# Attention of a gated cross-attention block in half-precision pairs, exponentials head by head in 5 of 8 tiles, and one reordering in the gate phase

## The chip, the cores and the metric

The kernel runs on one core of one Trainium2 chip. The time is the device time of that core in microseconds (us). TensorE does matmuls and transposes, VectorE and ScalarE read what it leaves in PSUM, GpSimd works from SBUF alone, and SyncE issues the DMAs. In the rows they are PE (its weight loads PEld), DVE, ACT, POOL and SP.

## What is computed

The reference, cut to what matters. B = 4 batches of S = 1024 tokens, hidden size 512, 16 heads of 64; the context has 64 rows, so a token scores 16 x 64 = 1024 context entries.

```
def attention(query, key, value, w_q, w_k, w_v, w_o):
    q, k, v = (split_heads(t @ w) for t, w in ((query, w_q), (key, w_k), (value, w_v)))
    scores = jnp.einsum('bhqd,bhkd->bhqk', q, k) * HEAD_DIM ** (-0.5)
    scores = scores + (1.0 - mask)[None, None, :, :] * -10000.0      # causal
    weights = jax.nn.softmax(scores, axis=-1)
    return merge_heads(jnp.einsum('bhqk,bhkd->bhqd', weights, v)) @ w_o

def ffn(x, w_gate, w_up, w_down):       # x and every intermediate rounded to 16-bit steps
    up, gate = act_qdq(x @ lpbq_dequant(w_up).T), act_qdq(x @ lpbq_dequant(w_gate).T)
    o = act_qdq(act_qdq(gate * fixed_qdq_u16(sigmoid(gate))) * up)
    return o @ lpbq_dequant(w_down).T   # lpbq_dequant: 4-bit steps, blocks of 32

x = x + tanh(g_xattn) * attention(layernorm(x), ctx, ctx, w_q, w_k, w_v, w_o)
x = x + tanh(g_ffn) * ffn(layernorm(x), w_gate, w_up, w_down)
```

## The kernel before

There are four phases one behind the other, with a barrier or a grid-wide maximum between them: front (attention), gate, up, down. Each product is made of three matmuls in which both factors are split in a high and a low part (high x high, high x low, low x high). In the front the parts are fp32r, in the other phases fp16.

**Front.** The 4096 tokens are 32 tiles of 128 (index j, eight to a batch). Key weights times query weights are folded into A (512 x 1024), value weights times output weights into V, once for a batch; `Ah`, `Al`, `Vh`, `Vl` are their parts. All engines walk the same list of steps k (`schedule`), three of them software-pipelined over the tiles:

- PE in step k: eight transposes of the probabilities of tile k-2 into `pT` (L987), the 24 matmuls of the scores of tile k (L956), four transposes of the normalised input of tile k+1 (L974), and the 24 matmuls of the output of tile k-2 (L925). In steps 8 and 9 of a batch the A and V of the next batch are made between these (L891, L905).
- ACT in step k: `pTh` of tile k-2 (L631), the normalisation of tile k+2 (L616), one exponential over 128x1024 of tile k-1 (L655), `xh` of tile k+1 (L662), and the second normalisation of tile k-3.
- DVE in step k, inside a run of batches: statistics of tile k+2 (L750), `pTl` of tile k-2 (L798), largest score of each head of tile k-1 (L740), scores minus largest (L744), residual and its statistics for tile k-3 (L761, L767), sums of the exponentials (L775) and their reciprocals (L778), `xl` of tile k+1 (L859), largest of tile k-3 (L782). In the last batch the residual and its statistics come ahead of the largest score.
- POOL in step k: inverse deviations (L584 to L589), then probabilities of tile k-1 (L601).

Besides, four of the weight tiles of the gate matrix are dequantised in each of the first three batches (jobs q = 0 to 3). `job_scale` (DVE, L282 to L274) runs in steps 3 to 6, behind `xl`; `job_integer` (DVE, L324) and `job_turn` (PE, L333) in steps 4 to 7, `job_turn` behind `xl` of tile k+1; `job_hi` (ACT) and `job_lo` (DVE) in steps 5 to 8. PE may overwrite the scores in `pS` of tile k-2 when DVE has subtracted (`sub_done`). DVE, ACT and PE take their instructions strictly in this written order.

**Gate.** Four groups of 1024 tokens, each with two halves t of 12 products `it` of 12 matmuls (L1278). ACT empties each product (L1171), DVE takes its minimum and maximum (L1202, L1203). The weight tiles of the other matrices are dequantised meanwhile, one for each four products: at `it == 9` DVE runs `job_scales` for three coming tiles (L296 to L274), which is followed by `job_integer` of the tile in hand (L324); PE turns that tile behind product 11 (L333), which waits for it. `job_scales` runs in seven of the eight halves.

**Up and down** are not touched.

Of the kernel before, what the change touches and what calls it, by code (L numbers as in the profile page):

```python
# [26 lines left out]
P = 128  # L27
# [39 lines left out]
def flamingo_block(nc, x, ctx, g_xattn, g_ffn, w_q, w_k, w_v, w_o, w_gate, w_up, w_down, out):  # L67
# [22 lines left out]
    with ExitStack() as top:  # L90
# [49 lines left out]
        with ExitStack() as ff:  # L140
# [12 lines left out]
            with ExitStack() as early:  # L153
                Ah = sb(early, "Ah", [P, KT, INNER], F32R)
                Al = sb(early, "Al", [P, KT, INNER], F32R)

# [31 lines left out]

ROUNDS = 4


# [188 lines left out]
def front_phase(mk, xf, cf, weights, shared, g_xattn, g_ffn, w_src, w_dst, load_gate, unit, xr, xr_in, front_out, pS, pG, x1_d, xn_d, ident, mask, half,  # L380
# [13 lines left out]
    with ExitStack() as ph:  # L394
        xin = [sb(ph, f"xin{n}", [P, H], F32) for n in range(BQ)]
        xn = [sb(ph, f"xn{n}", [P, H], F32) for n in range(2)]
        xh = [sb(ph, f"xh{n}", [P, H], F32R) for n in range(2)]
        xl = [sb(ph, f"xl{n}", [P, H], F32R) for n in range(2)]
        pr = [sb(ph, f"pr{n}", [P, INNER], F32) for n in range(2)]
        pTh = sb(ph, "pTh", [P, INNER], F32R)  # L400
        pTl = sb(ph, "pTl", [P, INNER], F32R)
        x1 = [sb(ph, f"x1{n}", [P, H], F32) for n in range(2)]
# [8 lines left out]
        ssum = sb(ph, "ssum", [P, 2, HEADS], F32)  # L411
        srec = sb(ph, "srec", [P, 2, HEADS], F32)
        pT = pb(ph, "pT", 1024)
        pX = pb(ph, "pX")
# [10 lines left out]
        Vh = sb(ph, "Vh", [P, PAIRS, H], F32R)  # L425
        Vl = sb(ph, "Vl", [P, PAIRS, H], F32R)
        pw = [pS[0][:, 0:512], pS[0][:, 512:1024]]
# [14 lines left out]

        kbd_set, vb_set = sem("kbd_set"), sem("vb_set")
        apart_p, apart_e = sem("apart_p"), sem("apart_e")
        masked, apart, sx_red, sx_spread, sx_scale = (sem(n) for n in ("masked", "apart", "sx_red", "sx_spread", "sx_scale"))
# [164 lines left out]
        def _(act):  # L610
# [7 lines left out]
            def step(b, k, have, jobs):  # L618
# [7 lines left out]
                if have(k - 2):  # L626
                    j = k - 2
                    act.wait_ge(*tile(o_ps, b, j - 1))
                    for h, cs in enumerate(halves):
                        act.wait_ge(*part(pT_ps, b, j, h))  # L630
                        act.activation(pTh[:, cs], pT[:, cs], ACT.Copy).then_inc(pTh_done, 1)  # L631
                if q is not None and which != 0:
                    job_hi(act, J, b, q)

                def chunk_high(n):
                    act.wait_ge(*at(ch_ps, NCH * b, NCH * ahead + 8 * which + n + 1))
                    if which == 0:
                        act.activation(Ah[:, n // 2, halves[n % 2]], bank_of(k, 0, n), ACT.Copy, scale=SCALE).then_inc(ch_hi, 1)
                    else:
                        act.activation(Vh[:, block_of(n), :], bank_of(k, 1, n), ACT.Copy).then_inc(ch_hi, 1)  # L640

# [9 lines left out]
                def exponentials():  # L651
                    if have(k - 1):
                        j = k - 1
                        act.wait_ge(*tile(sub_done, b, j))
                        act.activation(pr[j % 2][:, :], pr[j % 2][:, :], ACT.Exp).then_inc(exp_done, 1)  # L655

                def high():
                    if have(k + 1):
                        j = k + 1
                        act.wait_ge(*tile(xT_ps, b, j))  # L660
                        act.wait_ge(*tile(s_ps, b, j - 2))
                        act.activation(xh[j % 2][:, :], pX[:, :], ACT.Copy).then_inc(xh_done, 1)  # L662

# [46 lines left out]
        def _(dve):  # L710
            def chunk_low(b, k, ahead, which, n):
                dve.wait_ge(*at(ch_hi, NCH * b, NCH * ahead + 8 * which + n + 1))
                bank = bank_of(k, which, n)
                if which == 0:
                    cs = halves[n % 2]
                    dve.scalar_tensor_tensor(out=Al[:, n // 2, cs], in0=bank, scalar=SCALE, in1=Ah[:, n // 2, cs].bitcast(F32),
                                             op0=ALU.mult, op1=ALU.subtract).then_inc(ch_lo, 1)
                else:
                    q = block_of(n)
                    dve.tensor_tensor(Vl[:, q, :], bank, Vh[:, q, :].bitcast(F32), ALU.subtract).then_inc(ch_lo, 1)  # L720

            def scores_down(b, j, between=lambda: None):
# [4 lines left out]
                dve.wait_ge(*tile(s_ps, b, j))  # L727
                dve.wait_ge(*part(pT_ps, b, j - 2, 1))
# [27 lines left out]
            def residual(b, j):  # L756
# [3 lines left out]
                dve.wait_ge(*tile(x2_done, b, j - 2))  # L760
                dve.scalar_tensor_tensor(out=x1[n][:, :], in0=pO[:, :], scalar=TG_X, in1=xin[j % BQ][:, :],  # L761
                                         op0=ALU.mult, op1=ALU.add).then_inc(x1_done, 1)
# [9 lines left out]
            def sums(b, j):  # L772
                n = j % 2
                dve.wait_ge(*tile(exp_done, b, j))
                dve.tensor_reduce(ssum[:, n, :], pr[n][:, :].rearrange("p (h c) -> p h c", c=CK), X, ALU.add).then_inc(sum_done, 1)  # L775
                dve.wait_ge(*tile(sum_done, b, j))
# [3 lines left out]
            def largest(b, j):  # L780
                dve.wait_ge(*tile(x2_done, b, j))
                dve.tensor_reduce(xmx[:, bass.ds(BQ * b + j, 1)], x2[j % 2][:, :], X, ALU.max,  # L782
                                  apply_absolute_value=True).then_inc(x2max_done, 1)

            def step(b, k, have, jobs):
# [7 lines left out]
                def lows():  # L793
                    if have(k - 2):
                        j = k - 2
                        for h, cs in enumerate(halves):
                            dve.wait_ge(*part(pTh_done, b, j, h))
                            dve.tensor_tensor(pTl[:, cs], pT[:, cs], pTh[:, cs].bitcast(F32), ALU.subtract).then_inc(pTl_done, 1)  # L798

# [15 lines left out]

                q = job_at(k, jobs, 2)
                if which == 0:
                    sums_up()
# [36 lines left out]
                if have(k + 1):  # L855
                    j = k + 1
                    dve.wait_ge(*tile(xh_done, b, j))
                    dve.wait_ge(*tile(s_ps, b, j - 2))
                    dve.tensor_tensor(xl[j % 2][:, :], pX[:, :], xh[j % 2][:, :].bitcast(F32), ALU.subtract).then_inc(xl_done, 1)  # L859
                some(8)  # L860
                q = job_at(k, jobs, 0)
                if q is not None:
                    job_scale(dve, J, b, q, unit[:, 3 * q + b:3 * q + b + 1])
                if have(k - 3):
                    largest(b, k - 3)

            for j in range(2):
                statistics(0, j)
            schedule(dve, step, straight=True)

# [10 lines left out]
        @block.tensor  # L881
        def _(pe):
            def keys(b, k, ahead, n):

                pe.wait_ge(*at(ch_lo, NCH * b, NCH * ahead + n - 3))
                if n == 0:
                    pe.wait_ge(kbd_set, 2 * b + 2 * ahead + 2)
                    pe.wait_ge(*tile(sub_done, b, k - 2))
                for q in range(4):
# [20 lines left out]
            def values(b, k, have, turn_x):  # L910
# [7 lines left out]
                for i in range(PAIRS):  # L918
# [18 lines left out]
                    if which == 1 and i % 2 == 1:  # L937
                        if i == 3:

                            pe.wait_ge(*tile(sub_done, b, k - 1))  # L940
                        four_heads(b, k, ahead, i // 2)

            def scores(b, k):
                pe.wait_ge(*tile(xl_done, b, k))
                pe.wait_ge(*tile(sub_done, b, k - 2))
                if k % BQ == 2:

                    pe.wait_ge(*at(ch_lo, NCH * b, NCH * (k // BQ) + NCH))
                for kt in range(KT):
# [4 lines left out]
                    for xs, As in ((xh, Ah), (xh, Al), (xl, Ah)):  # L954
                        for hf in range(2):
# [3 lines left out]
                                           stop=(kt == KT - 1 and xs is xl))  # L959
                mm.then_inc(s_ps, 1)  # L960

            def step(b, k, have, jobs):
# [30 lines left out]
                if k % BQ != 2 and not (which == 0 and have(k - 2)):  # L993
                    turn_x()
                values(b, k, have, turn_x)
                if which == 0:
                    scores(b, k)
# [36 lines left out]
            for r in range(ROUNDS):  # L1034
                project(wv, r, wv_in, [(k_sb, 3 + r)] if r < 2 else [(v_sb, r - 1)], v_ps)
            schedule(pe, step)

# [9 lines left out]
def gate_phase(mk, xn_d, xr, xr_in, front_out, pX, x_d, x_pair, gate_d, wsc, w_src, W, w_in, load_w, row_unit, row_scale, ident, S_X, INV_X, GPOS, GNEG):  # L1047
# [3 lines left out]
    with ExitStack() as ph:  # L1051
# [133 lines left out]
        def _(dve):  # L1185
# [668 lines left out]
```

## Time and profile before

| | us |
|---|---|
| median of 3 runs | 1414.65 |
| lowest, highest | 1409.73, 1418.82 |
| the profiled execution | 1419.34 |
| its span in the profile | 1417.6 |

| engine | busy, us | share of the span |
|---|---|---|
| PE | 1288.8 | 91% |
| PEld | 768.2 | 54% |
| DVE | 1008.7 | 71% |
| ACT | 663.8 | 47% |
| POOL | 243.2 | 17% |

All times of rows are of one profiled execution, counted from the start of its span. A matmul's duration (390 to 417 ns for 512 columns) is longer than the distance to the next one, since matmuls are pipelined; for what one costs, take the distance of starts. An ACTIVATE too starts before the record of the one ahead has ended. "x2" in a row means two instructions merged, with their joint duration.

### The profile page before, as it was taken

To read this page: it belongs to the slowest core of one execution; us is meant where nothing else is said; L and a number is where in the kernel's file an instruction comes from. 1 tells how busy PE (TensorE), PEld (TensorE's weight loads), DVE (VectorE), ACT (ScalarE), POOL (GpSimd) and SP (SyncE) were. 2 spreads that over 40 slices of the span, in tenths; PEclk is the share of its full clock that TensorE was granted. 3 is DMA by queue.
4 is the path that set the end of the run, shared out by engine and by line. 5 is a ranking of instruction groups with operands and counts; after the bars stand their busy time and mean duration, and the time that the engine had idled before them with its cause. 6 is when DMAs were issued, how large, how long until landed. Compare 5 with 4: busy or idle time off the path is not lost. (4 is left out here: it accounts for less than half of the span.)

```text
span 1417.6 us, 19287 instructions
## 1 busy us (share of the span) xinstructions
PE 1288.8 (91%) x6269; PEld 768.2 (54%) x6269; DVE 1008.7 (71%) x1465; ACT 663.8 (47%) x782; POOL 243.2 (17%) x331
## 2 busy tenths in 40 slices
PE   7899999999999989899998999999993039999998
PEld 6688868878878754444444444444441014444443
DVE  0478779878876656666656669997999994545554
ACT  3434344443443223333333268875677984343431
POOL 1124234324313221110011113210110000000000
PEclk9999999999999999999999999999997569999999
DMA  8013212212203355545553489974457863454543
GB/s 326 1 34 94 83 52 75 96 44 83 95 37 105 119 191 181 166 168 192 170 178 119 159 298 351 322 282 146 140 195 299 314 245 126 164 180 155 183 158 116
DMA packets 111244, 228.28 MB, mean 161 GB/s; under 512 B 23121, under 2 KB 35409, under 8 KB 111185
## 3 DMA queue, kind: packets, MB, share of 16 engines
q1 hardware_dynamic: 110896, 227.58, 46.8%
q8 instruction: 26, 0.43, 0.1%
q14 instruction: 34, 0.27, 0.1%
q10 hardware_dynamic: 288, 0.00, 0.0%
HBM read 136.32 MB, written 91.23 MB: 161 GB/s over the span
## 5 line engine op out<-in xcount | busy, mean ns | idle before, releaser
L1278 PE MATMUL gpG<-xph,Wh 128*128 128x512 f16 x384 | 149.3, 389 | 1.1 <-DVE xpl L1189 1.0
L1278 PE MATMUL gpG<-xpl,Wh 128*128 128x512 f16 x384 | 149.2, 388 | 0.0
L1278 PE MATMUL gpG<-xph,Wl 128*128 128x512 f16 x384 | 148.7, 387 | 0.0
L1801 PE MATMUL pD<-Wh,xph 128*128 128x512 f16 x384 | 145.5, 379 | 1.0 <-DVE xpl L1776 1.0
L1278 PE MATMUL pU<-xph,Wh 128*128 128x512 f16 x384 | 145.5, 379 | 0.0
L1278 PE MATMUL pU<-xpl,Wh 128*128 128x512 f16 x384 | 145.5, 379 | 0.0
L1278 PE MATMUL pU<-xph,Wl 128*128 128x512 f16 x384 | 145.5, 379 | 0.0
L1801 PE MATMUL pD<-Wl,xph 128*128 128x512 f16 x384 | 145.5, 379 | 0.0
L1801 PE MATMUL pD<-Wh,xpl 128*128 128x512 f16 x384 | 145.5, 379 | 0.0
L1171 ACT ACTIVATE gst<-gpG,rw 128x512 f32<-128x512 f32 x96 | 66.2, 689 | 161.8 <-PE gpG L1278 161.8
L1202 DVE TENSOR_REDUCE gmx<-gst 128x512 f32 (+1 forms) x96 | 65.6, 684 | 97.9 <-ACT gst L1171 97.7
L925 PE MATMUL pO<-Vh,pTh 128*128 128x512 f32 x256 | 106.7, 417 | 3.5 <-DVE pTl L798 2.3
L925 PE MATMUL pO<-Vh,pTl 128*128 128x512 f32 x256 | 101.3, 396 | 0.0
L925 PE MATMUL pO<-Vl,pTh 128*128 128x512 f32 x256 | 101.1, 395 | 0.0
L956 PE MATMUL pS<-Ah,xh 128*128 128x512 f32 x256 | 81.7, 400 | 1.7 <-DVE Vl L720 1.7
L956 PE MATMUL pS<-Al,xh 128*128 128x512 f32 x256 | 79.4, 391 | 0.0
L956 PE MATMUL pS<-Ah,xl 128*128 128x512 f32 x256 | 79.0, 390 | 0.0
L631 ACT ACTIVATE pTh<-pT 128x512 fp32r<-128x512 f32 x64 | 34.8, 597 | 93.0 <-PE pT L987 93.0
L1419 ACT ACTIVATE gb<-nq,sc 128x1536 f32<-128x1536 int16 x48 | 75.2, 1568 | 4.4 <-POOL nq L1399 4.2
L1292 PE MATMUL pD<-ident 128*128 128x512 f16 x28 | 7.9, 446 | 75.5 <-DVE pmx L1714 75.5
L601 POOL TENSOR_TENSOR pr<-pr,srec 128x1024 f32<-128x1024 f32 x32 | 61.0, 1906 | 72.8 <-DVE srec L778 72.4
L655 ACT ACTIVATE pr<-pr 128x1024 f32<-128x1024 f32 x32 | 33.9, 1060 | 82.9 <-DVE pr L744 62.2
(222 smaller groups left out, 2639.5 us busy)
## 6 DMA issues: line engine op xcount, KB each, us to landing
dub<-up_d SPq DMA_DIRECT2D x42, 768.0 KB, 4.8
gate_d<-gst SPq DMA_DIRECT2D x96, 256.0 KB, 2.0
gb<-gate_d SPq DMA_DIRECT2D x24, 768.0 KB, 6.5
up_d<-ust SPq DMA_DIRECT2D x72, 256.0 KB, 4.2
eu<-up_d SPq DMA_DIRECT2D x22, 768.0 KB, 6.1
xr<-xn_d SPq DMA_DIRECT2D x9, 1024.0 KB, 6.0
xin<-in_x SPq DMA_DIRECT2D x32, 256.0 KB, 2.8
x_d<-x SPq DMA_DIRECT2D x32, 256.0 KB, 2.0
```

The source lines that it names most:

```text
L601: pool.tensor_tensor(p3, p3, srec[:, j % 2, :].unsqueeze(2).to_broadcast([P, HEADS, CK]), ALU.mult).then_inc(prob_done, 1)
L631: act.activation(pTh[:, cs], pT[:, cs], ACT.Copy).then_inc(pTh_done, 1)
L655: act.activation(pr[j % 2][:, :], pr[j % 2][:, :], ACT.Exp).then_inc(exp_done, 1)
L925: mm = pe.matmul(pO[:, :], ps_[:, cs], vs[:, p, :], start=(i == 0 and ps_ is pTh and vs is Vh), stop=(i == PAIRS - 1 and ps_ is pTl))
L956: mm = pe.matmul(pS[k % 2][:, hf * 512:(hf + 1) * 512], xs[k % 2][:, cs], As[:, kt, hf * 512:(hf + 1) * 512], start=(kt == 0 and xs is xh ...
L1171: act.activation(stage[n][:, :], pG[m % 3][:, :], ACT.Copy, scale=row_scale[0][:, it:it + 1]).then_inc(g_sb, 1)
L1202: dve.tensor_reduce(gmx[:, 1, bass.ds(2 * IT * i + m, 1)], stage[m % NS][:, :], X, ALU.min).then_inc(g_neg, 1)
L1278: mm = pe.matmul(ps[:, :], Ws[:, it, kt * P:(kt + 1) * P], xs[:, kt, :], start=(kt == 0 and Ws is Wh and xs is xh), stop=(kt == KT - 1 and ...
L1292: pe.matmul(ps, words[:, 0:P], words.unsqueeze(1).to_broadcast([P, 2, 2 * P]), start=True, stop=True)
L1419: act.activation(gb[k % NG][:, :], nq[:, k % QT, :], ACT.Sigmoid, scale=S_G).then_inc(sig_done, 1)
L1801: mm = pe.matmul(pD[4 * t + q][:, :], os_[n][:, cs], Ws[:, it, :], start=(it == 0 and os_ is oh and Ws is Wh), stop=(it == IT - 1 and os_ ...
```

## The change

1. `Ah`, `Al`, `Vh`, `Vl`, `xh`, `xl`, `pTh`, `pTl` become fp16. So that they fit, each is multiplied by a power of two: x by 2^10, probabilities by 2^14, A and V by 2^15 over a power-of-two unit that bounds their largest possible entry. The scale is undone in the scale of the exponential (`S_UNIT`) and of the residual (`O_SCALE`). The subtractions on DVE become `scalar_tensor_tensor` with the same operands.
2. The units are found at the start: `largest_of` (DVE) over `wq`, `kT`, `wo`, `vT`, `spread_bounds` (PE, two small transposes each), and `fit_in`, `fit_a`, `fit_v`, chains of ten and nine small DVE instructions. The first high part of A and of V waits for them.
3. In tiles 2 to 6 of each batch (steps 3 to 7) DVE no longer subtracts and no longer sums: it takes the negated largest scores, multiplies these 16 columns by `S_UNIT`, and ACT runs 16 exponentials of 128x64 from `pS`, each with a column of bias, a column of scale, and a sum over its head (`accum_out`). PE overwrites `pS` only when these are done.
4. In the gate phase `job_integer` runs at `it == 9` without `job_scales` ahead of it; `job_scales` moves to `it == 10`.

```
+X_TOP, P_TOP, M_TOP = 2.0 ** 10, 2.0 ** 14, 2.0 ** 15
-                Ah = sb(early, "Ah", [P, KT, INNER], F32R)
+                Ah = sb(early, "Ah", [P, KT, INNER], F16)
...
+        def by_heads(j):
+            return j % BQ in range(2, 7)
...                                                                   # ACT
+                    if not jobs and b == 0 and ahead == 0 and n == 0:
+                        act.wait_ge(v_fit if which else a_fit, 1)
...
                         act.wait_ge(*tile(sub_done, b, j))
-                        act.activation(pr[j % 2][:, :], pr[j % 2][:, :], ACT.Exp).then_inc(exp_done, 1)
+                        if not by_heads(j):
+                            act.activation(pr[n][:, :], pr[n][:, :], ACT.Exp, scale=S_UNIT).then_inc(exp_done, 1)
+                            return
+                        act.wait_ge(*part(pT_ps, b, j - 2, 1))
+                        for h in range(HEADS):
+                            at_pr = h % 2 * PAIRS + h // 2
+                            e = act.activation(pr[n][:, at_pr * CK:(at_pr + 1) * CK], pS[n][:, h * CK:(h + 1) * CK], ACT.Exp,
+                                               bias=smx[:, n, h:h + 1], scale=S_UNIT, accum_out=ssum[:, n, at_pr:at_pr + 1])
+                        e.then_inc(exp_done, 1)
...                                                                   # DVE
+                elif by_heads(j):
+                    dve.tensor_reduce(smx[:, n, :], s3, X, ALU.max, negate=True).then_inc(max_done, 1)
+                    dve.wait_ge(*tile(max_done, b, j))
+                    dve.tensor_scalar(smx[:, n, :], smx[:, n, :], S_UNIT, None, ALU.mult).then_inc(sub_done, 1)
...
+                if by_heads(j):
+                    dve.sem_inc(sum_done, 1)
+                else:
+                    dve.tensor_reduce(ssum[:, n, :], pr[n][:, :].rearrange("p (h c) -> p h c", c=CK), X, ALU.add).then_inc(sum_done, 1)
...
+                if k == 0:
+                    dve.wait_ge(v_sb, ROUNDS)
+                    largest_of(3, flat(vT))
...
+                if k == 0:
+                    fit_v()
...                                                                   # DVE, ahead of the steps
+            largest_of(0, flat(wq))
             for j in range(2):
                 statistics(0, j)
+            dve.wait_ge(k_sb, ROUNDS)
+            largest_of(1, flat(kT))
+            dve.wait_ge(id_set, 2)
+            fit_a()
+            dve.wait_ge(wo_in, 16)
+            largest_of(2, flat(wo))
...                                                                   # PE
+                pe.wait_ge(*tile(exp_done if by_heads(j) else sub_done, b, j))
...                                                                   # DVE, gate phase
-                        if it == 9 and t == 0:
-                            job_scales(dve, J, i, 3, row_unit[2][:, bass.ds(i, 1)])
-                        if it == 9 and t == 1 and not last:
-                            job_scales(dve, J, i, 6, row_unit[1][:, bass.ds(3 * i + 3, 3)])
                         if it % 4 == 1:
                             job_integer(dve, J, i, q, (10 * i, 5 * t + 5))
+                        if it == 10 and t == 0:
+                            job_scales(dve, J, i, 3, row_unit[2][:, bass.ds(i, 1)])
+                        if it == 10 and t == 1 and not last:
+                            job_scales(dve, J, i, 6, row_unit[1][:, bass.ds(3 * i + 3, 3)])
```

## Rows read from the trace of the kernel before

**Rows 1.** Busy time by stretch: columns PE, PEld, DVE, ACT, POOL, PEclk, DMA, GB/s

```profile
80.00:480.00 400.00, 397.05 (x2040) 319.41 (x2039) 317.12 (x536) 155.42 (x238) 135.40 (x218) 1.00 0.23 75
500.00:820.00 320.00, 295.37 (x1424) 147.00 (x1423) 200.32 (x366) 114.27 (x184) 44.70 (x54) 0.97 0.51 173
```

**Rows 2.** Waits of PE over the span: us in total, times, longest

```profile
PE gjbank L333 <- DVE gjd L324: 20.1, 7, 3.6
```

**Rows 3.** Timeline of PE, one step of the last batch: start us, us

```profile
443.30 1.04 PE L987 MATMUL pT<-ident,pr 128*128 128x128 f32 x8
...
446.94 0.62 PE L956 MATMUL pS<-Ah,xh 128*128 128x512 f32 x2
...
449.21 0.62 PE L956 MATMUL pS<-Ah,xl 128*128 128x512 f32 x2
...
450.33 0.40 PE L925 MATMUL pO<-Vl,pTh 128*128 128x512 f32 x1
...
455.48 0.40 PE L925 MATMUL pO<-Vh,pTl 128*128 128x512 f32 x1
455.71 1.04 PE L987 MATMUL pT<-ident,pr 128*128 128x128 f32 x8
```

**Rows 4.** Timeline of PE, fp16 matmuls of the gate phase

```profile
600.43 0.38 PE L1278 MATMUL gpG<-xph,Wh 128*128 128x512 f16 x1
...
605.83 0.38 PE L1278 MATMUL gpG<-xpl,Wh 128*128 128x512 f16 x1
```

**Rows 5.** Timeline of PE, starts of steps 3 and 7 of a batch with jobs

```profile
201.30 1.03 PE L987 MATMUL pT<-ident,pr 128*128 128x128 f32 x8
...
252.23 1.04 PE L987 MATMUL pT<-ident,pr 128*128 128x128 f32 x8
```

**Rows 6.** Timeline of DVE from step 3 of that batch

```profile
202.57 1.29 DVE L798 TENSOR_TENSOR pTl<-pT,pTh 128x512 fp32r<-128x512 f32 x2 [2.14 <-ACT pTh L631]
203.77 1.22 DVE L740 TENSOR_REDUCE smx<-pS 128x16 f32<-128x1024 f32 x1
...
206.16 0.74 DVE L761 SCALAR_TENSOR_TENSOR x<-pO,sc,xin 128x512 f32<-128x512 f32 x1
...
207.88 1.19 DVE L775 TENSOR_REDUCE ssum<-pr 128x16 f32<-128x1024 f32 x1
...
209.81 0.67 DVE L282 TENSOR_REDUCE pjmx<-pjw 128x16 f32<-128x512 f32 x1
...
213.56 0.68 DVE L750 BATCH_NORM_STATS2 st<-xin 128x6 f32<-128x512 f32 x1
```

**Rows 7.** Timeline of POOL in that step

```profile
209.44 1.91 POOL L601 TENSOR_TENSOR pr<-pr,srec 128x1024 f32<-128x1024 f32 x1
```

**Rows 8.** Groups of ACT by shape: busy us, mean ns of one

```profile
L616 ACT ACTIVATE xn<-xin,rs 128x512 f32<-128x512 f32 x32 | 26.0, 815 | 29.8 <-POOL rs L589 29.8
L631 ACT ACTIVATE pTh<-pT 128x512 fp32r<-128x512 f32 x64 | 34.8, 597 | 93.0 <-PE pT L987 93.0
L655 ACT ACTIVATE pr<-pr 128x1024 f32<-128x1024 f32 x32 | 33.9, 1060 | 82.9 <-DVE pr L744 62.2 <-DVE pr L738 20.8
```

**Rows 9.** Timeline of ACT at the start, pairs of instructions in a row

```profile
9.48 0.19 ACT L690 ACTIVATE sc<-sc 128x1 f32<-128x1 f32 x1
9.58 0.19 ACT L691 ACTIVATE sc<-sc 128x1 f32<-128x1 f32 x1
...
36.69 1.52 ACT L616 ACTIVATE xn<-xin,rs 128x512 f32<-128x512 f32 x2
```

**Rows 10.** Timeline of DVE around one `job_scales` of the gate phase

```profile
550.79 1.86 DVE L296 TENSOR_REDUCE gjmx<-gjw 128x16 f32<-128x512 f32 x3
...
553.65 0.15 DVE L264 TENSOR_SCALAR gjrm<-gjrm 128x1 f32<-128x1 f32 x1 [0.15 <-DVE gjrm L262]
...
554.93 1.06 DVE L324 TENSOR_TENSOR gjd<-gjq,gjsn 128x512 f32<-128x512 int16 x1
```

**Rows 11.** Granted clock right behind that wait: columns as in rows 1

```profile
555.90:559.10 3.20, 3.05 (x10) 1.61 (x11) 3.07 (x6) 0.60 (x1) 2.76 (x4) 0.50 0.05 13
```

More of the change, by code:

```diff
@@ L396, in front_phase @@
         xn = [sb(ph, f"xn{n}", [P, H], F32) for n in range(2)]
-        xh = [sb(ph, f"xh{n}", [P, H], F32R) for n in range(2)]
-        xl = [sb(ph, f"xl{n}", [P, H], F32R) for n in range(2)]
+        xh = [sb(ph, f"xh{n}", [P, H], F16) for n in range(2)]
+        xl = [sb(ph, f"xl{n}", [P, H], F16) for n in range(2)]
         pr = [sb(ph, f"pr{n}", [P, INNER], F32) for n in range(2)]
-        pTh = sb(ph, "pTh", [P, INNER], F32R)
-        pTl = sb(ph, "pTl", [P, INNER], F32R)
+        pTh = sb(ph, "pTh", [P, INNER], F16)
+        pTl = sb(ph, "pTl", [P, INNER], F16)
         x1 = [sb(ph, f"x1{n}", [P, H], F32) for n in range(2)]
@@ L412, in front_phase @@
         srec = sb(ph, "srec", [P, 2, HEADS], F32)
+        bounds = sb(ph, "bounds", [P, 4], F32)
+        wide = sb(ph, "wide", [P, 4], F32)
+        fit = sb(ph, "fit", [P, 16], F32)
+        (A_TOP, A_T, A_UNIT, A_INV, A_SCALE, S_UNIT, S_SCALE, V_TOP, V_T, V_UNIT, V_INV, V_SCALE, V_BACK, O_SCALE) = (
+            fit[:, n:n + 1] for n in range(14))
         pT = pb(ph, "pT", 1024)
@@ L443, in front_phase @@
         kbd_set, vb_set = sem("kbd_set"), sem("vb_set")
+        bound_done, bound_ps, fit_link, a_fit, v_fit = (sem(n) for n in ("bound", "bound_ps", "fit_link", "a_fit", "v_fit"))
         apart_p, apart_e = sem("apart_p"), sem("apart_e")
@@ L630, in step @@
                         act.wait_ge(*part(pT_ps, b, j, h))
-                        act.activation(pTh[:, cs], pT[:, cs], ACT.Copy).then_inc(pTh_done, 1)
+                        act.activation(pTh[:, cs], pT[:, cs], ACT.Copy, scale=P_TOP).then_inc(pTh_done, 1)
                 if q is not None and which != 0:
@@ L661, in high @@
                         act.wait_ge(*tile(s_ps, b, j - 2))
-                        act.activation(xh[j % 2][:, :], pX[:, :], ACT.Copy).then_inc(xh_done, 1)
+                        act.activation(xh[j % 2][:, :], pX[:, :], ACT.Copy, scale=X_TOP).then_inc(xh_done, 1)
                 def normal2():
@@ L783, in largest, with link, largest_of, fit_in @@
                                   apply_absolute_value=True).then_inc(x2max_done, 1)
+            seq = [0]
+            def link(ins):
+                seq[0] += 1
+                ins.then_inc(fit_link, 1)
+                dve.wait_ge(fit_link, seq[0])
+            def largest_of(n, data):
+                dve.tensor_reduce(bounds[:, n:n + 1], data, X, ALU.max, apply_absolute_value=True).then_inc(bound_done, 1)
+            def fit_in(top, t, unit, inv, n, terms):
+                dve.wait_ge(bound_ps, n // 2 + 1)
+                link(dve.tensor_reduce(wide[:, n:n + 2], pO[:, 0:2 * P].rearrange("p (a k) -> p a k", a=2), X, ALU.max))
+                link(dve.tensor_scalar(top, wide[:, n:n + 1], wide[:, n + 1:n + 2], terms, ALU.mult, ALU.mult))
+                link(dve.tensor_scalar(top, top, TINY, None, ALU.max))
+                link(dve.tensor_scalar(t, top, 2.0 ** 23 + 1.0, None, ALU.mult))
+                link(dve.tensor_scalar(unit, top, -(2.0 ** 23), t, ALU.mult, ALU.add))
+                link(dve.reciprocal(inv, unit))
+            def flat(t):
+                return t[:, :, :].rearrange("p a b -> p (a b)")
+            def fit_a():
+                fit_in(A_TOP, A_T, A_UNIT, A_INV, 0, HD)
+                link(dve.tensor_scalar(S_UNIT, A_UNIT, SCALE / (M_TOP * X_TOP), None, ALU.mult))
+                link(dve.tensor_scalar(S_SCALE, A_INV, M_TOP * X_TOP / SCALE, None, ALU.mult))
+                link(dve.tensor_scalar(mask[:, :], mask[:, :], S_SCALE, None, ALU.mult))
+                dve.tensor_scalar(A_SCALE, A_INV, M_TOP, None, ALU.mult).then_inc(a_fit, 1)
+                dve.wait_ge(a_fit, 1)
+            def fit_v():
+                dve.wait_ge(tanh_done, 2)
+                fit_in(V_TOP, V_T, V_UNIT, V_INV, 2, HD)
+                link(dve.tensor_scalar(V_BACK, V_UNIT, 1.0 / (M_TOP * P_TOP), None, ALU.mult))
+                link(dve.tensor_scalar(O_SCALE, TG_X, V_BACK, None, ALU.mult))
+                dve.tensor_scalar(V_SCALE, V_INV, M_TOP, None, ALU.mult).then_inc(v_fit, 1)
+                dve.wait_ge(v_fit, 1)
             def step(b, k, have, jobs):
@@ L797, in lows @@
                             dve.wait_ge(*part(pTh_done, b, j, h))
-                            dve.tensor_tensor(pTl[:, cs], pT[:, cs], pTh[:, cs].bitcast(F32), ALU.subtract).then_inc(pTl_done, 1)
+                            dve.scalar_tensor_tensor(out=pTl[:, cs], in0=pT[:, cs], scalar=P_TOP, in1=pTh[:, cs],
+                                                     op0=ALU.mult, op1=ALU.subtract).then_inc(pTl_done, 1)
                 def down(between=lambda: None):
@@ L887, in keys @@
                     pe.wait_ge(kbd_set, 2 * b + 2 * ahead + 2)
-                    pe.wait_ge(*tile(sub_done, b, k - 2))
+                    scores_read(b, k - 2)
                 for q in range(4):
@@ L944, in scores @@
                 pe.wait_ge(*tile(xl_done, b, k))
-                pe.wait_ge(*tile(sub_done, b, k - 2))
+                scores_read(b, k - 2)
                 if k % BQ == 2:
@@ L960, in scores, with spread_bounds @@
                 mm.then_inc(s_ps, 1)
+            def spread_bounds(n):
+                pe.wait_ge(bound_done, n + 2)
+                for a in range(2):
+                    mm = everywhere(pe, pO[:, a * P:(a + 1) * P], bounds[:, n + a:n + a + 1], ident)
+                mm.then_inc(bound_ps, 1)
             def step(b, k, have, jobs):
```

34 lines of the change are left out of this document (22 added, 12 removed).

## The prediction, as put on record

> **What bounds the kernel now.** I read first the busy time by stretch. In the front, from 80 to 480 us, PE is busy for 397 of 400 us at the full clock (1.00, its level of 2.4 GHz), DVE for 317, ACT for only 155 [rows 1]; in the gate phase, 500 to 820 us, PE is busy for 295 of 320 and the clock is 0.97 on average. So PE sets the pace in both, and in the gate phase it is kept waiting. The table of PE's waits says by whom: 20.1 us, seven times, for the dequantised tile of `job_integer` [rows 2]. Then I read PE's timeline for what a step of the front takes, and last the timelines of the engines that PE would wait for if it were quicker. The up and down phases aren't touched and nothing in them is costed.
>
> **fp16 on PE.** The reader is to look at distances of starts. Scores: from 446.94 to 449.21 us there are ten fp32r matmuls, 227 ns each; output: from 450.33 to 455.48 twenty-two, 234 ns [rows 3]. In the gate phase 25 fp16 matmuls of the same shape take 5.40 us, 216 ns each [rows 4]. A tile has 24 of either kind: 24 x 11 + 24 x 18 ns = 0.7 us off a step that takes 12.41 us (443.30 to 455.71) [rows 3]. So PE alone could take 11.75 us; with the 0.44 us of a `job_turn` 12.2 instead of 12.85, which is what steps 3 to 7 give before (50.93 us for one step without and three with it) [rows 5]. Over 32 tiles that is 21 us, if nothing else is in the way. The conversions on ACT and DVE keep their operand counts and sizes; the weight loads were hidden and stay so.
>
> **DVE loses, ACT gains work.** In 20 of the 32 tiles DVE drops the subtraction (maximum and subtraction together take from 203.77 to 206.16, 2.39 us, of which the maximum is 1.22) and the sums (1.19) [rows 6], 2.35 us; a multiplication of 16 columns comes in, about 0.3 us with its wait, as a link of `job_scales` has 0.15 of idle before it and lasts 0.15 [rows 10]. ACT drops one exponential of 1.06 us [rows 8] and takes 16 small ones. This price decides the case, and no row has that form. Its nearest: two normalisations with a column of bias and a column of scale take 1.52 us together [rows 9] and one alone 0.815 [rows 8], so the second starts 0.705 after the first, for 512 columns. Columns cost (1060 - 597)/512 = 0.9 ns each by the two copies and exponentials at hand [rows 8]; 448 fewer make 0.705 - 0.39 = 0.31, a little less from PSUM: 0.30 us. That is without the sum over the head. Reading the sum out can't be seen in the trace: from below nothing (0.30), in the middle one more slot of ACT, as the two 128x1 instructions that start 0.10 apart (9.48, 9.58), from above the whole 0.19 of one of these [rows 9], 0.49. I take 0.40, since a value that leaves the engine by itself is most like an instruction of one column. So 16 exponentials are 6.4 us (4.8 to 7.8) where 1.06 stood.
>
> The Trainium skill, page "ScalarE: Activation LUTs", section "What ACT_TABLE_LOAD costs", gives 280 ns + 0.833 ns a column with a bias pointer, 93 more for a second pointer, and an overlap of 93: 333 ns for 64 columns, and no price for the sum. By that figure alone the sixteen would be 5.3 us, the front would lose 19 us instead of the 40 worked out below, and the kernel would come to about 1408.
>
> **What the 6.4 us lie on.** DVE and ACT can't overlap here as before: DVE's reciprocal waits for the last exponential, and behind it stand, in DVE's written order, everything up to the next maximum, which the next exponentials wait for. ACT's `xh` is queued behind the exponentials too, DVE's `xl` behind `xh`, and PE's `job_turn` waits for `xl`. Round from one tile's exponentials to the next, in steps with jobs: `xh` 0.55, `xl` 0.6, `job_scale` and the largest of the tile (209.81 to 213.56) 3.75, statistics 0.98 (as their twin, 1.72 from 206.16 to 207.88 less 0.74), `pTl` 1.20 (202.57 to 203.77), maximum 1.25, small multiplication 0.3, hand-over 0.1: 8.7; and 6.4 for ACT: 15.1 us, with `job_lo` (0.6, from step 5 on) 15.7 [rows 6]. DVE's residual, its statistics and `job_integer` fit beneath the exponentials and cost nothing. PE needs 12.2: it waits. In step 3 and in the last batch, without jobs, another round is the longer one: from PE's transposes to the end of `pTl` 2.47 (201.30 to 203.77) [rows 5, 6], maximum, multiplication, hand-over 1.6, exponentials 6.4, reciprocal 0.4, GpSimd's probabilities 1.91 and its signal 2.0 [rows 7]: 12.85; in the last batch residual and statistics (1.72) come ahead of the maximum: 14.55.
>
> Against before: in a batch with jobs step 3 +0.4, step 4 +2.25, steps 5 to 7 +2.85 each, steps 8 to 10 about -0.5 each for fp16 (DVE and ACT, making A and V, leave not all of the 0.7): +9.7, three times 29. Last batch: 5 x (14.55 - 12.41) = +10.7. Steady front: +40 us. Each 0.01 us on one exponential is 20 x 0.16 = 3.2 us; at 0.30 the front loses 8, at 0.49 69. fp16 alone, with DVE's work of before, would not give the 21 either: in a job step DVE's rows follow one another from 202.57 to 213.56 without a gap [rows 6], so PE could not have drawn away from it.
>
> **The start.** The maxima over `wq`, `kT`, `wo` run while DVE has nothing else. The one over `vT`, 2048 columns, comes ahead of the statistics of tile 2, whose normalisation stands ahead of the first parts of A on ACT: at 1.2 ns a column (1.22 us for 1024) 2.4 us on the path [rows 6]. `fit_v`, nine small links of 0.3 [rows 10], delays the first tile's mask by about 1.2 of its 3 us. Less the fp16 of the first steps (3 x 0.3): +2.5 us.
>
> **The gate phase.** At `it == 9` `job_scales` stands from 550.79 to 554.93, 4.1 us, ahead of `job_integer` [rows 10]; PE waits for its tile seven times, as often as `job_scales` runs. After the change its tile is ready 4.1 us earlier, more than the longest of the waits, 3.6. So the whole 20.1 us go [rows 2]. Behind such a wait the granted clock fell to 0.50 (1.2 GHz) for 555.9 to 559.1 us [rows 11]; the mean of 0.97 over 320 us is 9.6 us of full clock lost [rows 1], of which about 1.6 belong to the start of the phase: 8 us more. `job_scales` at `it == 10` holds back the extremes of product 11 and `job_lo` by some 4 us; ACT needs that buffer four products (10 us) later, and the next tile is turned 13 us later, so it is covered. Sum: -28 us.
>
> **Sum.** 40 + 2.5 - 28 = +14.5 us on the profiled execution's own 1419.34 (span 1417.6, 1.7 outside): 1433.8. The median of the runs is 4.7 lower, 1414.65, and so the forecast is 1429 for it.
>
> **Rivals.**
> 1. Reading the sum is free, one exponential takes 0.30 us: the front loses 8, not 40, and the kernel is faster: 1414.65 + 8 + 2.5 - 28 = 1397. It decides from 0.31 us down (below 1400.5); at 0.355 gain and loss cancel. For it: ACT has 245 of 400 us idle, and the pointers' price is well read. Against: a sum has to leave the engine somehow.
> 2. The sum empties ACT's pipeline each time, 0.49 us: +69, 1458.
> 3. The gate phase doesn't get its wait back, because `job_integer` then waits for GpSimd or PE for `job_lo`: +28, 1457. Against: GpSimd is busy for 45 of 320 us there [rows 1].
> 4. PE's new waits in the front, 1.5 to 2.8 us, bring the half clock as the ones in the gate phase did: the last batch above all, with one wait of 2.8 a step. Transposes at half clock add 0.9 to the round, five times, and perhaps as much in job steps: +5 to +20, 1434 to 1449.
> 5. PE doesn't profit from fp16: the steps that are bound elsewhere hide it; +5, 1434.
>
> **Chances.** Forecast, with 0.36 to 0.45 us an exponential: 0.45, its own range 1416 to 1446. Rival 1: 0.25. Rival 2: 0.10. Rival 3: 0.06. Rival 4: 0.10. Rival 5: 0.04. The range has to reach from rival 1 to the edge of rivals 2 and 3: 1394 to 1454. This kernel can be told from no change at about 1%, 14 us. Below 1400.5 lies most of rival 1, 0.22; up to 1428.8 its rest and somewhat under half of the forecast's case, 0.30; above it 0.48.
>
> **What would show it.** The start-to-start distance of the 16 exponentials, 0.40; steps 4 to 7 of a batch 15.1 to 15.7 us apart and the last batch's 14.5, with PE waiting for `prob` and `job_turn` for `xl`; fp16 matmuls 216 ns apart in the front; no wait of PE at L333 in the gate phase, and its clock at 1.00. The prediction is wrong if an exponential takes 0.31 us or less, if the gate phase keeps its waits, or if DVE's order lets more pass beneath the exponentials than I laid there.

## The result, and the profile after

| | us |
|---|---|
| changed kernel, median of 4 runs | 1427.27 (1424.93 to 1427.79) |
| kernel before, median of 4 runs on the same chip | 1416.18 (1409.73 to 1418.82) |
| ratio | 1.0082, 95% interval 1.0044 to 1.0119 |
| span of the profiled execution, before and after | 1417.6 and 1423.2 |

The kernel became 0.8% slower. Forecast were 1429 and a range of 1394 to 1454.

The span grew by 5.6 us, and two large changes of opposite sign make it up. The first view is that of all instructions on the gate phase's product tile: durations, then first and last start. Before the change:

```profile
L1278 PE MATMUL gpG<-xph,Wh x384: 379/379/634, 518.0 to 820.2; 128*128 128x512 f16 x192
```

After it:

```profile
L1384 PE MATMUL gpG<-xph,Wh x384: 379/379/389, 555.4 to 825.9; 128*128 128x512 f16 x192
```

The front ends 37.4 us later (518.0 to 555.4), and the gate phase takes 270.5 us from first to last start instead of 302.2, 31.7 us less. From there on both kernels run alike.

PE's waits after the change: us in total, times, longest. The row of [rows 2], 20.1 us for the dequantised tile, is gone; these have come or grown (the last stood at 2.6 us, once, before):

```profile
PE pT L1089 <- POOL pr L612: 20.1, 20, 2.7
PE pX L334 <- DVE xl L938: 15.5, 12, 1.6
PE pO L1020 <- DVE x L789: 4.5, 9, 0.8
PE pT L1000 <- DVE Vl L742: 3.7, 4, 2.8
```

Twenty waits for probabilities, one for each tile done head by head, and twelve for `xl`, one for each `job_turn` of the front. Busy time by stretch, columns as in [rows 1], the second stretch being the gate phase:

```profile
80.00:480.00 400.00, 364.55 (x1915) 190.51 (x1914) 267.28 (x495) 235.92 (x734) 126.59 (x208) 0.98 0.21 67
555.00:826.00 271.00, 270.53 (x1354) 135.45 (x1355) 191.09 (x349) 109.05 (x178) 39.68 (x48) 1.00 0.59 196
```

In the front PE is busy for 365 of 400 us where it was 397, though DVE has become much freer (317 to 267) and ACT is at 236. No engine is full: they take turns. In the gate phase PE is full and its granted clock is back at 1.00 from 0.97. The transposes that open steps 3 to 7 of the second batch with jobs, in PE's timeline (start, duration):

```profile
211.25 1.04 PE L1089 MATMUL pT<-ident,pr 128*128 128x128 f32 x8
224.12 1.09 PE L1089 MATMUL pT<-ident,pr 128*128 128x128 f32 x8 [1.04 <-POOL pr L612]
238.74 1.09 PE L1089 MATMUL pT<-ident,pr 128*128 128x128 f32 x8 [0.42 <-POOL pr L612]
253.94 1.97 PE L1089 MATMUL pT<-ident,pr 128*128 128x128 f32 x8 [0.51 <-POOL pr L612]
```

The distances are 12.9, 14.6 and 15.2 us. Before, the step without a `job_turn` took 12.41 us and one with it 12.84 (50.93 us for the four of [rows 5]). Now the three engines of the round, in step 3. ACT's exponentials and the reading of their sums, first and last:

```profile
215.32 0.41 ACT L675 ACTIVATE pr<-pS,smx,fit 128x64 f32<-128x64 f32 x1 [1.65 <-DVE smx L766]
215.62 0.19 ACT L675 ACTIVATION_READ_ACCUMULATOR pr<-pS,smx,fit 128x1 f32 x1
215.71 0.40 ACT L675 ACTIVATE pr<-pS,smx,fit 128x64 f32<-128x64 f32 x1
...
221.34 0.27 ACT L675 ACTIVATION_READ_ACCUMULATOR pr<-pS,smx,fit 128x1 f32 x1
221.44 0.66 ACT L684 ACTIVATE xh<-pX 128x512 f16<-128x512 f32 x1
```

ACTIVATION_READ_ACCUMULATOR is the reading of the sum. One exponential and its reading take 0.38 us from start to start (0.29 and 0.09), sixteen 6.12 us (215.32 to 221.44). DVE meanwhile:

```profile
213.72 1.22 DVE L764 TENSOR_REDUCE smx<-pS 128x16 f32<-128x1024 f32 x1
214.97 0.23 DVE L766 TENSOR_SCALAR smx<-smx,fit 128x16 f32<-128x16 f32 x1
...
221.83 0.25 DVE L809 RECIPROCAL srec<-ssum 128x16 f32<-128x16 f32 x1 [4.92 <-DVEq L804]
222.13 0.69 DVE L938 SCALAR_TENSOR_TENSOR xl<-pX,xh 128x512 f16<-128x512 f32 x1
222.74 0.67 DVE L283 TENSOR_REDUCE pjmx<-pjw 128x16 f32<-128x512 f32 x1
...
228.41 1.22 DVE L764 TENSOR_REDUCE smx<-pS 128x16 f32<-128x1024 f32 x1
```

and GpSimd:

```profile
222.17 1.90 POOL L612 TENSOR_TENSOR pr<-pr,srec 128x1024 f32<-128x1024 f32 x1 [3.80 <-DVE srec L809]
```

DVE stands idle for 4.92 us ahead of the reciprocal, which waits until the last exponential is done (DVEq is DVE's own sequencer, which passes that signal on), and then has 6.3 us of work (222.13 to 228.41) before the next maximum, on which ACT waits. In the kernel before DVE's rows from 202.57 to 213.56 us [rows 6] follow one another with 0.9 us of idle in all, no piece of it over 0.15; now one engine waits while the other works.

### The profile page after: what moved, and what is told of

It reads as the page before. It is cut to its first block and busy times, and to the rows that moved or that the text cites. A ratio compares the mean times of both kernels' runs of the same rounds, so it can differ in the third digit from the quotient of the medians.

```text
span 1423.2 us, 19941 instructions
## 1 busy us (share of the span) xinstructions
PE 1271.0 (89%) x6273; PEld 635.2 (45%) x6273; DVE 985.0 (69%) x1468; ACT 772.0 (54%) x1402; POOL 236.2 (17%) x331
## 5 line engine op out<-in xcount | busy, mean ns | idle before, releaser
L1384 PE MATMUL gpG<-xph,Wh 128*128 128x512 f16 x384 | 145.6, 379 | 1.1 <-DVE xpl L1295 1.0
L1384 PE MATMUL gpG<-xpl,Wh 128*128 128x512 f16 x384 | 145.5, 379 | 0.0
L675 ACT ACTIVATE pr<-pS,smx,fit 128x64 f32<-128x64 f32 x320 | 124.1, 430 | 32.7 <-DVE smx L766 32.7
L1020 PE MATMUL pO<-Vh,pTh 128*128 128x512 f16 x256 | 97.5, 381 | 7.4 <-DVE x L789 4.5
L1020 PE MATMUL pO<-Vl,pTh 128*128 128x512 f16 x256 | 97.1, 379 | 0.0
L1020 PE MATMUL pO<-Vh,pTl 128*128 128x512 f16 x256 | 97.0, 379 | 0.0
L1051 PE MATMUL pS<-Ah,xh 128*128 128x512 f16 x256 | 79.5, 393 | 3.0 <-DVE Vl L742 3.0
L1051 PE MATMUL pS<-Al,xh 128*128 128x512 f16 x256 | 78.6, 389 | 0.0
L1051 PE MATMUL pS<-Ah,xl 128*128 128x512 f16 x256 | 78.0, 387 | 0.0
L809 DVE RECIPROCAL srec<-ssum 128x16 f32<-128x16 f32 x32 | 8.1, 253 | 98.5 <-DVEq L804 98.1
```

The lines of the kernel that those rows point to most:

```text
L675: e = act.activation(pr[n][:, at_pr * CK:(at_pr + 1) * CK], pS[n][:, h * CK:(h + 1) * CK], ACT.Exp, bias=smx[:, n, h:h + 1], scale=S_UNIT, ...
L809: dve.reciprocal(srec[:, n, :], ssum[:, n, :]).then_inc(rec_done, 1)
L1020: mm = pe.matmul(pO[:, :], ps_[:, cs], vs[:, p, :], start=(i == 0 and ps_ is pTh and vs is Vh), stop=(i == PAIRS - 1 and ps_ is pTl))
L1051: mm = pe.matmul(pS[k % 2][:, hf * 512:(hf + 1) * 512], xs[k % 2][:, cs], As[:, kt, hf * 512:(hf + 1) * 512], start=(kt == 0 and xs is xh ...
L1384: mm = pe.matmul(ps[:, :], Ws[:, it, kt * P:(kt + 1) * P], xs[:, kt, :], start=(kt == 0 and Ws is Wh and xs is xh), stop=(kt == KT - 1 and ...
```

## The experiments

Each was run in three rounds beside the kernel before; ratios carry 95% intervals. "Changed kernel" is the one above. The kernel before had a median of 1417.69 us beside experiments 1 to 4 and 1414.74 beside 5 to 8; differences between versions are taken from their medians in us and can be off by these 3 us where the sets differ.

**1. The gate phase's reordering alone.** The kernel before with this edit:

```
-                        if it == 9 and t == 0:
+                        if it == 10 and t == 0:
                             job_scales(dve, J, i, 3, ...)
...     # likewise t == 1; both behind job_integer
```

> The kernel before with the gate phase's reordering alone. My theory (PE's seven waits for the dequantised tile and the half clock behind five of them were caused by job_scales standing ahead of job_integer): the gate phase shrinks by 28 to 32 us, so 1385 +- 4, 0.978 of before; no wait of PE on the tile is left. Rival (the gate phase of the changed kernel is shorter because of something the front left behind, such as the clock or the DMA load): less than 10 us here.

Measured: 1388.45 us, ratio 0.9799 (0.9782 to 0.9816), 29 us less than the 1417.69 of before beside it; the gate phase from first to last start 271.1 us:

```profile
L1278 PE MATMUL gpG<-xph,Wh x384: 379/379/634, 518.1 to 789.2; 128*128 128x512 f16 x192
```

The time is within the interval expected, and PE's waits for the dequantised tile are gone. The front is unchanged there, so what the gate phase wins doesn't come from the front.

**2. The changed kernel with that edit undone.**

```
-                        if it == 10 and t == 0:
+                        if it == 9 and t == 0:
                             job_scales(dve, J, i, 3, ...)
...     # likewise t == 1; both ahead of job_integer
```

> The changed kernel with job_scales back ahead of job_integer. Theory: it loses what the gate phase had won, 28 to 32 us, 1458 +- 4, 1.030 of before; front the same as in the changed kernel. Rival (the two parts interact): another difference to the changed kernel than e1_gate_only has to the kernel before.

Measured: 1457.09 us, ratio 1.0283 (1.0266 to 1.0300), so 39 us slower than before. The wait of [rows 2] is back as it was, and the gate phase lasts 301.4 us from first to last start:

```profile
PE gjbank L334 <- DVE gjd L325: 20.1, 7, 3.6
L1384 PE MATMUL gpG<-xph,Wh x384: 379/379/634, 556.3 to 857.7; 128*128 128x512 f16 x192
```

With the -29 of experiment 1 that makes +10, and the changed kernel itself has +11: the two parts add up.

**3. No tile head by head.** The changed kernel with:

```
-            return j % BQ in range(2, 7)
+            return False
```

> The changed kernel with no tile done head by head: fp16 pairs, the fits at the start and the gate reordering stay. Theory (the 16 exponentials with their sums, on the round DVE - ACT - DVE, cost 40 us of the front, and fp16 gives some 11, because DVE is nearly full in the job steps): front 45 us shorter than in the changed kernel, 1380 +- 6, steps with jobs 12.2 to 13.3 us apart, the last batch's 11.75. Rival A (fp16 itself or the fits cost the front time, for instance by slower conversions): over 1400. Rival B (fp16 gives all of its 21 us): 1370.

Measured: 1376.91 us, ratio 0.9715 (0.9696 to 0.9734): 50 us less than the changed kernel, and 11.5 less than experiment 1, which differs from it by the fp16 pairs and the fits alone. PE's timeline, steps 3 to 7 of the batch:

```profile
199.78 1.04 PE L1089 MATMUL pT<-ident,pr 128*128 128x128 f32 x8
211.45 1.04 PE L1089 MATMUL pT<-ident,pr 128*128 128x128 f32 x8
223.55 1.04 PE L1089 MATMUL pT<-ident,pr 128*128 128x128 f32 x8
236.20 1.04 PE L1089 MATMUL pT<-ident,pr 128*128 128x128 f32 x8
249.37 1.04 PE L1089 MATMUL pT<-ident,pr 128*128 128x128 f32 x8
```

11.67, 12.10, 12.65 and 13.17 us: PE is the bound in the first two, and then DVE, filled by the jobs (11.85 us busy in the step of 12.65, 11.94 in that of 13.17), falls behind and holds it up. PE's waits for the residual from 80 to 500 us:

```profile
PE pO L1020 <- DVE x L789: 8.4, 12, 1.3
```

Rival A falls (the time is under 1400). Of rival B's 21 us 11.5 were had net, with some 3 us of later start against them; the other 7 or so are where the expectation put them, in the steps in which DVE is nearly full.

**4. `job_scale` beneath the exponentials.** The changed kernel, DVE's order in every step:

```
+                q = job_at(k, jobs, 0)
+                if q is not None:
+                    job_scale(dve, J, b, q, unit[:, 3 * q + b:3 * q + b + 1])
                 if have(k - 1):
                     sums(b, k - 1)
...
                 some(8)
-                q = job_at(k, jobs, 0)
-                if q is not None:
-                    job_scale(dve, J, b, q, unit[:, 3 * q + b:3 * q + b + 1])
```

> The changed kernel with job_scale moved in DVE's order to a place ahead of the reciprocal, so that its 3.15 us run beneath ACT's exponentials. Theory (what costs is that DVE and ACT take turns, not ACT's amount of work): steps 4 to 7 of the batches with jobs fall from 14.6-15.2 to 12.5-13.2 us, 27 us in all, 1400 +- 5; the last batch stays at 14.6 a step. Rival (ACT's own work of about 9.5 us a step plus its waits is the bound): under 8 us gained, 1420 or more.

Measured: 1405.48 us, ratio 0.9919 (0.9902 to 0.9936), 22 us less than the changed kernel (half a microsecond outside what was expected). ACT and DVE do exactly the same work as before this edit; only the order differs. Steps of the batch:

```profile
203.85 1.04 PE L1089 MATMUL pT<-ident,pr 128*128 128x128 f32 x8
216.72 1.09 PE L1089 MATMUL pT<-ident,pr 128*128 128x128 f32 x8 [1.04 <-POOL pr L612]
229.58 1.09 PE L1089 MATMUL pT<-ident,pr 128*128 128x128 f32 x8 [0.42 <-POOL pr L612]
243.03 1.09 PE L1089 MATMUL pT<-ident,pr 128*128 128x128 f32 x8 [0.52 <-POOL pr L612]
```

12.87, 12.86, 13.45 us. Steps 4 to 7 lost 1.75 us each, not the 3.15 of `job_scale`. I put that down to the next round, from PE's transposes over DVE, ACT and GpSimd back to them: steps 3 and 4 are now as long as step 3 was with the changed kernel (12.87), steps 5 to 7 are longer by the 0.6 us of `job_lo`, and every step opens with a wait for the probabilities. That round was not shortened here by itself; experiment 5 does it in the last batch. The rival (ACT's amount of work) falls.

**5. The same, and in the last batch the residual behind the maximum.**

```
-                    early = which is not None or not have(BQ)
+                    early = which is not None or (not have(BQ) and not by_heads(k - 1))
```

> e4_scale_early, and in the last batch the residual and its statistics go behind the largest score in the tiles that are done head by head. Theory (there the round from PE's transposes over DVE, ACT and GpSimd back to the next transposes sets the step, and the residual's 1.7 us lie on it): the last batch's steps fall from 14.6 to 12.9 us, 8 to 9 us in all, 1397 +- 4. Rival (in the last batch PE's half clock or ACT's work sets the step): under 3 us.

Measured: 1393.35 us, ratio 0.9851 (0.9829 to 0.9874), 12 us less than experiment 4. The last batch's steps:

```profile
446.20 1.09 PE L1089 MATMUL pT<-ident,pr 128*128 128x128 f32 x8 [1.03 <-POOL pr L612]
459.11 1.09 PE L1089 MATMUL pT<-ident,pr 128*128 128x128 f32 x8 [1.03 <-POOL pr L612]
472.03 1.09 PE L1089 MATMUL pT<-ident,pr 128*128 128x128 f32 x8 [1.03 <-POOL pr L612]
```

12.9 us each, as expected, 1.7 less, which is 8.5 us in five steps. Most of what exceeds them is the clock. With PE's waits of 2.7 us gone no stretch at the half clock is left in the front's batches, where experiment 4 had three in its last batch, and the longest shows what it cost: the same step in experiment 4 (granted clock 0.68 on average) and in this one, columns as in [rows 1]:

```profile
508.07:518.80 10.73, 9.12 (x32) 3.98 (x33) 5.94 (x10) 2.93 (x4) 2.90 (x4) 0.68 0.64 212
497.86:505.74 7.88, 6.27 (x33) 3.28 (x33) 5.94 (x10) 2.93 (x4) 2.91 (x4) 1.00 0.56 195
```

That is 2.85 us; two earlier steps at the half clock, 15.28 and 14.88 us instead of 14.6, make another 0.9. The clock was not changed by itself, so that the shorter waits are what kept it up is argued from the rows.

**6. Exponentials head by head, sums by DVE.** The changed kernel with:

```
-                                               bias=smx[:, n, h:h + 1], scale=S_UNIT, accum_out=ssum[:, n, at_pr:at_pr + 1])
+                                               bias=smx[:, n, h:h + 1], scale=S_UNIT)
...
-                if by_heads(j):
-                    dve.sem_inc(sum_done, 1)
-                else:
+                if True:
                     dve.tensor_reduce(ssum[:, n, :], ...)
```

> The changed kernel, with the exponentials head by head but without their sums; DVE sums them in one instruction as in the kernel before. Theory (reading out a sum costs ACT 0.093 us, sixteen of them 1.49 us on the round; DVE's sum puts 1.2 there instead): each of the 20 rounds 0.3 us shorter, 6 us in all, 1421 +- 4; exponentials 0.29 us apart. Rival (taking the sum costs nothing beyond its record): exponentials stay 0.38 apart and the kernel gets slower by 20 times 1.2, 1450.

Measured: 1418.08 us, ratio 1.0019 (1.0000 to 1.0038), 9 us less than the changed kernel. ACT's timeline, fourteen of the exponentials in one merged row:

```profile
213.87 4.24 ACT L675 ACTIVATE pr<-pS,smx,fit 128x64 f32<-128x64 f32 x14
```

They are 0.29 us apart without the readings (13 distances and one duration of 0.4 to 0.5 make 4.24). The rival falls: the sum has a price of its own. Sixteen readings on ACT (16 x 0.093 = 1.49 us) cost the round more than DVE's one sum does: each of the 20 rounds is 0.39 us shorter here (14.22 and 14.81 where 14.61 and 15.20 stood), 8 us in all, where 0.3 and 6 had been expected.

**7. Head by head alone, in fp32r.** The kernel before with the branches of `by_heads`, and

```
+                            e = act.activation(pr[n][:, at_pr * CK:(at_pr + 1) * CK], pS[n][:, h * CK:(h + 1) * CK], ACT.Exp,
+                                               bias=smx[:, n, h:h + 1], scale=1.0, accum_out=ssum[:, n, at_pr:at_pr + 1])
```

> The kernel before (fp32r, gate phase as it was) with tiles 2 to 6 of a batch head by head, scale an immediate and no multiplication of the 16 columns. Theory (each column pointer of an ACTIVATE costs 0.09 us): the exponentials are 0.29 us apart instead of 0.38, the rounds of steps 4 to 7 are 12.8 to 13.9 us, and the front loses only 5 to 10 us, 1424 +- 4. Rival (the second pointer is free): 0.38 apart, +30 us or more, 1448.

Measured: 1428.33 us, ratio 1.0094 (1.0071 to 1.0117), just above the interval expected. ACT's timeline in a tile done head by head:

```profile
218.82 0.31 ACT L666 ACTIVATE pr<-pS,smx 128x64 f32<-128x64 f32 x1
219.03 0.19 ACT L666 ACTIVATION_READ_ACCUMULATOR pr<-pS,smx 128x1 f32 x1
219.12 0.31 ACT L666 ACTIVATE pr<-pS,smx 128x64 f32<-128x64 f32 x1
```

The exponential starts some 0.2 us before its reading, and the next 0.09 after that (0.196 and 0.093 in the trace's nanoseconds): 0.289 in all, against 0.382 with a column as scale. So the second column pointer is not free, and the rival falls. The row of the gate phase's product tile shows that the front ends 5.7 us later than before (518.0 to 523.7):

```profile
L1303 PE MATMUL gpG<-xph,Wh x384: 379/379/634, 523.7 to 828.8; 128*128 128x512 f16 x192
```

and the gate phase, the same code as before, took 305.1 instead of 302.2 in this execution, with one stretch at the half clock twice as long as the others. That makes 8.6 of the 13.6 us. The other 5 are mostly the choice of execution: the profiled one of the kernel before, 1419.34 us, lies 4.6 above the median of 1414.74 that stood beside this set.

**8. No tile head by head, and the residual ahead of the maximum everywhere.** Experiment 3 with:

```
-                    if early:
-                        sums_up()
+                    sums_up()
+                    if early:
                         spread2()
                     down()
                     if not early:
-                        sums_up()
                         spread2()
```

> e3_no_heads with the residual ahead of the largest score in every step, the order of the last batch. Theory (what PE still waits for in e3_no_heads, 8.4 us in the steps with jobs, is the residual, queued behind DVE's maximum and subtraction; DVE stays full in two of these steps): 3 us less than e3_no_heads, 1374 +- 2. Rival (DVE's amount of work in the job steps is the whole of it): no difference.

Measured: 1373.76 us, ratio 0.9709 (0.9688 to 0.9730), 3 us less than experiment 3 in another set of runs. The edit moves the residual alone and leaves its statistics where they were. Of the waits for the residual none is left; in their place stand shorter ones for the probabilities, in the steps in which DVE is nearly full:

```profile
PE pT L1088 <- POOL pr L612: 4.3, 6, 0.7
```

The rival, that DVE's amount of work is the whole of it, falls. This is the fastest of all versions, 41 us under the kernel before and 53 under the changed one.

## Why the prediction was right

**fp16 on PE: right.** The matmuls of the front are 216 ns apart, as those of the gate phase had been [rows 4]:

```profile
217.74 0.38 PE L1020 MATMUL pO<-Vh,pTh 128*128 128x512 f16 x1
...
222.70 0.38 PE L1020 MATMUL pO<-Vh,pTl 128*128 128x512 f16 x1
```

(23 distances in 4.96 us.) The step that PE alone sets came to 11.67 us in experiment 3; 11.75 was forecast. That part of this gain would be lost under DVE's load in the job steps also held: 11.5 us net instead of 21. (DVE's rows of before were not quite without a gap, as the forecast had it: they held 0.9 us of idle.)

**The price of an exponential: right, and the term that decided.** 0.382 us against the 0.40 taken; 0.289 without the sum against 0.30, one more slot of ACT of 0.093 against 0.10. The difference of 0.018, times 320, is 5.8 us.

**The rounds: right, a little long.** Forecast for steps 4 to 7 were 15.1 and 15.7, measured 14.6 and 15.2; 0.3 of the half microsecond are the cheaper exponentials. Step 3: 12.85 and 12.87. Last batch: 14.55 and 14.6. In these two the cheaper exponentials should have shown as well, so the rest of that round was read 0.3 us too short. Experiments 4 and 5 change nothing but DVE's order and shorten the steps by 1.75 and 1.7 us, which shows that taking turns was the cost, and experiment 3 that without the exponentials head by head the front loses nothing: +40 forecast, measured 37.4 at the end of the front less 3.3 of the start, 34. The gap has the size of the 5.8 us of the exponential, but it isn't that term alone. The three batches with jobs lost 23.3 us where 29 were forecast; of this gap some 4 us are the exponentials, and 0.9 is step 7, which had taken 13.15 us before and not the 12.85 of the working. The last batch lost 11.5 where 10.7 were forecast.

**The start: right in kind, short by 0.8.** The first transposes of probabilities start 3.3 us later than before, 2.5 were forecast. The maximum over `vT` stands where it was feared, and PE waits for what it delays:

```profile
46.31 2.28 DVE L826 TENSOR_REDUCE bounds<-vT 128x1 f32<-128x2048 f32 x1
```

PE's timeline behind it:

```profile
53.17 2.05 PE L986 MATMUL pS<-kbd,wqT 128*128 128x128 f32 x16 [2.43 <-DVE Al L738]
```

`fit_v` was cheaper than forecast, 2.1 us for the nine links. What the working had left out is that the scale of the first parts of A is now a column too, though it said that these instructions keep their operands: ACT takes 680 ns for one where it took 595, DVE 720 to 745 for `Al` where it took 670 to 690.

**The gate phase: right in its steps, mis-sized by 3 us.** -28 forecast; -31.7 in the span, -31.1 in experiment 1. The 20.1 us of [rows 2] are counted from the modelled end of a matmul, 0.16 us behind the point from which the next could start, seven times; and the loss by the half clock was worked out from a mean rounded to 0.97. A third piece is 1.4 us: the stretch at the half clock that opens the phase, which the forecast left standing. Before, it lasted from 518.2 to 521.6 us, inside the phase; in the changed kernel the clock was at 0.50 from 516.8 to 520.2, long before the phase starts at 555.

**The rivals.** Rival 1 (0.30 us) fell by the reading of the sum; rival 2 (0.49) likewise, since a reading holds ACT for 0.093 us and not for 0.19; rival 3 by experiment 1. Rival 4 is partly so: the clock fell in the front's batches, six times, but it cost little. The stretches around the two that begin in the batch shown, columns as in [rows 1]:

```profile
253.90:257.50 3.60, 3.56 (x13) 2.41 (x14) 2.80 (x11) 1.68 (x3) 1.87 (x4) 0.53 0.50 176
284.50:288.20 3.70, 3.70 (x18) 3.28 (x18) 2.18 (x4) 1.61 (x3) 0.00 (x0) 0.54 0.69 246
```

The first falls in a step in which PE waits anyway, and the step is no longer for it (15.20 us, as its neighbours). The second falls in a step that PE fills, which took 20.51 us where the same step of the other batches took 19.17: 1.3 us. The last batch lost 0.1 by one, and the other three left their steps as they were, so the clock cost some 1.4 us. In experiment 4's last batch it cost 3.8. Rival 5 would have had steps 8 to 10 gain nothing from fp16; they gained 0.8, 0.6 and 0.3 us (19.94 to 19.17, 17.65 to 17.02, 13.15 to 12.85) where 0.5 each was taken. So it fell, and that DVE's load eats fp16's gain in the job steps was in the forecast itself.

**Part of the agreement is luck.** The front was forecast at 42.5 and came to 37.4, the gate phase at -28 and came to -31.7: both misses point the same way, 5 and 4 us, and the span's +5.6 lies 9 under the +14.5 of the sum. The medians differ by 11 us where the two profiled spans differ by 5.6: the profiled execution before lies 3.2 above its median and the one after 2.3 below, within the scatter of the kernel before (1409.73 to 1418.82). That scatter goes with the clock: of the thirteen runs of the kernel before beside experiments 5 to 8 the fastest, 1409.46 us, had a mean granted clock of 0.970 and the slowest, 1420.78, one of 0.962, while the four runs of experiment 1 lie within 1.6 us. The forecast of 1429 is nearer to the median of 1427.27 than its terms deserve.

## What to carry to other kernels

Moving work from a full engine to a half-empty one helps only if it doesn't stand on a round in which the two wait for each other: ask for the length of the round, and what of the first engine's work can be written beneath the second's. Sixteen small instructions cost sixteen fixed prices, of each column pointer and each sum read out too; here 6.1 us replaced 1.06 on ACT to spare DVE 2.35. And before an engine is relieved by more work elsewhere, look for a wait that a swap of two calls removes: that one was worth 29 us, two and a half times the 11.5 that the pairs in fp16 gave.

## What the runs showed of the hardware

- Taking a sum along with an ACTIVATE shows as an instruction of its own, ACTIVATION_READ_ACCUMULATOR. It holds ACT for 93 ns, though its record lasts 190 to 270; the records of a row of sixteen grow longer (0.40 to 0.47 us for the exponentials) at unchanged distance.
- A column pointer costs ACT 93 ns: exponentials of 64 columns from PSUM start 289 ns apart with bias and scale as columns and 196 ns ahead of the next instruction with the bias alone. The exponentials over 128x1024 in the other twelve tiles, whose scale became a column, last 1148 ns where they lasted 1060. The Trainium skill, page "ScalarE: Activation LUTs", section "What ACT_TABLE_LOAD costs", gives the same 93 ns for a pointer; its 333 ns for the distance is 44 above the 289 measured from PSUM.
- A matmul of 512 columns with its own weights: 227 to 234 ns apart in fp32r [rows 3], 216 in fp16. The weight loads take 188 and 98 to 101 ns.
- PE's clock fell to half in the front without one long wait: in the step before 253.9 us the waits were 0.4 to 1.6 us each.
